# Routed attention in blocks of two rows of queries: 256 columns per instruction for values and sums

## The chip, the cores and the metric

One core of a Trainium2 chip runs the whole program. The metric is the time of one execution on the device in microseconds. Its engines are named as the profile names them: PE is TensorE (matmuls; PEld is its weight load), DVE is VectorE, ACT is ScalarE, POOL is GpSimd, SP is SyncE, which here only starts transfers.

## What is computed

The input x is 2 x 1024 tokens of 512 numbers. It is normalised, and two attentions are added to it: a local one with its own projections (16 query heads, 4 key heads, a window of 64 keys), and a routed one, which is what the change touches. In the routed attention each token has 16 query heads of 32 numbers but one key and one value only, those of the head that a gate picks:

```python
k_shared = einsum('bth,bthd->btd', indicator, k)
v_shared = einsum('bth,bthd->btd', gating_top1, v)
att = einsum('bhqd,bkd->bhqk', q, k_shared) * (1.0 / sqrt(32))
att = softmax(where(causal, att, -inf), axis=-1)
y = einsum('bhqk,bkd->bhqd', att, v_shared)
...
return x + local_attention(xn) + y
```

## The kernel before

The program has two stages. The first (0 to about 403 us) makes projections and the local attention of all tokens, 256 tokens a round. The second is the routed attention, from about 403 us to the end. It works through 8 units (`UNITS_ROUTED`), each a batch and a group of four heads (`HQ = 4`). A unit has 8 rows of queries, 128 queries each (`i`), against key blocks of 128 keys (`j`, up to `i`): 36 pairs, listed in `PRODUCTS` as (i, i), (i, 0), ..., (i, i-1).

For every unit PE does these kinds of work; the letters are used from here on.

- M, `row_scores` (L980): queries of one head by up to 512 keys into one of four PSUM banks (`s_ps`). DVE takes the causal maximum of each (L1250). There are 48 of them in a unit, written with 256, 384 or 512 columns. They are for the unit that comes next.
- ROW, `max_in_rows` (L994): once DVE has joined a unit's maxima (`row_maxima`, L1270 to L1275), PE turns them into a row, ACT copies it and sends it by DMA (L1452) into the rows of `q_op` under the queries. The key scores of that unit wait for it.
- S, `key_scores` (L1011): 128 keys by 4 heads x 128 queries, 512 columns, into one of three banks (`st_ps`). ACT takes the exponential (L1469) into one of 12 buffers (`p_t`, `RING`). On the diagonal POOL clears what is not causal (L1589); of two neighbouring pairs of a row POOL makes the sum (L1600, `PAIR_OF`), into one of 6 buffers (`p_sum`, `SUMS`).
- V, `key_values` (L1025): for one pair, four matmuls (one for each head, 32 output partitions each) of `v_all` with the weights, into the one bank `od_ps`, 128 columns.
- v, `key_sums` (L1039): the same with a block of ones in place of the values, for each sum of two pairs, at the end of a row. In this trace every matmul of V and v stands as two records, two passes for each operand of four bytes, and the four heads of a pass run side by side.
- F, `finish` (L1049): after ACT has copied `od_ps` (L1479), two transposes; DVE divides (L1287, L1289) and after rows 3 and 7 adds what the first stage left (L1296).

All engines run one list of steps in order. The class `Routed` writes that list by a model of its own: it keeps a time for each engine and always takes the step that could start first, in the order F, M or ROW, S, V where they tie. V goes in groups: `value_group` takes 4 pairs at once, or all that are left in the row if these are 5 or fewer, and the sums follow the row's last group. `TURN = 0.15` is what the model counts for entering and for leaving such a group. It counts 0.22 us for the four matmuls of one pair:

```python
        for g in range(k, k + value_group(k)):
            self.do("key_values", u, b, g)
            self.now += 0.22
```

No step waits out of order: what PE's list puts behind a ROW waits for that ROW. The functions that the diff touches:

## Time and profile before

| what | value |
|---|---|
| median of 3 runs | 728.02 us (725.67 to 728.77) |
| the profiled execution, its own time | 726.53 us |
| its span from first to last instruction | 725.1 us |
| mean granted clock of TensorE | 0.969 |
| first stage | to about 403 us |
| ROW of units 1 and 7 | 458.2 and 683.9 us |

The profile is one execution. A granted clock of 1.00 is 2.4 GHz, 0.50 is 1.2 GHz. In the timeline an entry may hold several instructions; the start of the next entry says when the engine went on, since busy times of pipelined matmuls overlap. In the order lists below one line is one run of like instructions.

### The profile page before, as it was taken

The numbers are of one execution on the slowest core, as the hardware profiler recorded it, in microseconds if no ns is written. First come the engines' busy times: TensorE is split into PE (matmuls) and PEld (weight loads), VectorE is DVE, ScalarE is ACT, GpSimd is POOL, SyncE is SP. The second block draws the span as 40 slices with busy tenths as digits, with TensorE's granted clock in tenths as the row PEclk, the third lists the DMA queues.
The fourth block names the chain that finished last, engine by engine and source line by source line (L and its number), as shares of the span: only waits on it lengthen the run. The fifth ranks groups of instructions, "written<-read, shape, count | busy, mean of one in ns | idle before, by whom it ended". The sixth has DMA issues, their size and how long they took to land. (4 is left out here: it accounts for less than half of the span.)

```text
span 725.1 us, 19425 instructions
## 1 busy us (share of the span) xinstructions
PE 660.7 (91%) x7433; PEld 522.8 (72%) x7433; DVE 528.7 (73%) x1376; ACT 365.0 (50%) x907; POOL 432.4 (60%) x352
## 2 busy tenths in 40 slices
PE   4796999899989999989988889899999999999997
PEld 3675887778877888778876567676767676667775
DVE  3975677577783777837865898898888888988621
ACT  4453454426545255443454235356556555656674
POOL 2963846285671856707752236466766666767696
PEclk9899999999999999989999789899999999999999
DMA  8412122232211322112116500311413130402011
GB/s 295 178 57 87 45 63 87 71 88 68 82 46 55 102 63 73 59 55 74 54 49 185 142 24 24 104 45 48 104 47 86 47 101 26 126 26 82 4 32 31
DMA packets 61451, 55.04 MB, mean 76 GB/s; under 512 B 5806, under 2 KB 52270, under 8 KB 61358
## 3 DMA queue, kind: packets, MB, share of 16 engines
q1 hardware_dynamic: 59096, 52.76, 24.4%
q8 instruction: 59, 0.97, 0.6%
q10 hardware_dynamic: 2262, 1.04, 0.5%
q14 instruction: 34, 0.28, 0.1%
HBM read 35.63 MB, written 17.89 MB: 74 GB/s over the span
## 5 line engine op out<-in xcount | busy, mean ns | idle before, releaser
L1250 DVE CUSTOM_DVE_ANT_0 s_ps<-s_ps,x_ln 128x512 f32<-128x512 f32 (+2 forms) x368 | 196.2, 589 | 34.0 <-PE s_ps L980 32.7
L862 PE MATMUL gemm<-w_tok,xt 128*128 128x512 f32 (+1 forms) x768 | 179.6, 382 | 4.7 <-DVE g_exp L1110 2.3
L862 PEld LDWEIGHTS gemm<-w_tok,xt 128*128 128x128 f32 x768 | 132.9, 194 | 29.8 <-DVE g_exp L1110 2.8
L980 PE MATMUL s_ps<-k_stack,w_tok 96*128 96x512 f32 (+2 forms) x368 | 117.9, 407 | 2.2 <-DVE picked_fk L1250 1.6
L1011 PE MATMUL st_ps<-w_tok,k_stack 98*128 98x512 f32 x288 | 105.1, 430 | 0.4 <-ACT qkv L1469 0.2
L1469 ACT ACTIVATE p_loc<-st_ps 128x512 f32<-128x512 f32 x144 | 77.8, 599 | 46.6 <-PE st_ps L1011 46.1
L980 PEld LDWEIGHTS s_ps<-k_stack,w_tok 96*128 96x128 f32 x368 | 65.4, 200 | 35.4 <-DVE picked_fk L1250 17.1
L1416 ACT ACTIVATE p_loc<-win,l_max 128x96 f32<-128x96 f32 x256 | 61.1, 391 | 12.4 <-DVE l_max L1195 12.4
L1547 POOL TENSOR_TENSOR rope_b<-qkv,sin_t 128x128 f32<-128x128 f32 (+1 forms) x32 | 27.4, 879 | 65.2 <-DVE qkv L1162 65.1
L1469 ACT ACTIVATE p_loc_t<-st_ps 128x512 f32<-128x512 f32 x96 | 52.2, 599 | 24.2 <-PE st_ps L1011 23.4
L1531 POOL TENSOR_TENSOR rms_y<-rms_v,minus_half 128x20 f32<-128x20 f32 x16 | 58.6, 3666 | 9.4 <-DVE rms_v L1172 9.4
L858 PE MATMUL gemm<-xt,w_qt 128*128 128x256 f32 x384 | 57.6, 296 | 5.4 <-DVE picked_fv L1141 3.4
L1011 PEld LDWEIGHTS st_ps<-w_tok,k_stack 98*128 98x128 f32 x288 | 52.4, 198 | 10.8 <-ACT p_loc L1469 2.3
L858 PEld LDWEIGHTS gemm<-xt,w_qt 128*128 128x128 f32 x384 | 51.0, 197 | 8.9 <-DVE picked_fv L1141 4.5
L1571 POOL TENSOR_TENSOR p_loc<-p_loc,l_rec 128x1536 f32<-128x1536 f32 x16 | 44.2, 2761 | 22.0 <-DVE l_rec L1207 22.0
L948 PE MATMUL gemm<-w_o,attn_t 128*128 128x512 f32 x192 | 50.5, 398 | 2.3 <-DVE x_res L1221 1.7
L1250 DVE DVE_READ_ACCUMULATOR2_ANT picked_fk<- 128x1 f32 x368 | 51.6, 140 | 0.0
L1589 POOL TENSOR_SCALAR_AFFINE_SELECT p_loc<-p_loc 128x512 f32<-128x512 f32 x40 | 25.3, 638 | 42.9 <-ACT p_loc L1469 42.8
L1425 ACT ACTIVATE p_loc_t<-win 96x512 f32<-96x512 f32 x64 | 37.5, 604 | 19.8 <-PE win L922 19.7
L922 PE MATMUL win<-idt,p_loc 128*96 128x128 f32 x256 | 40.9, 286 | 5.4 <-ACT p_loc L1416 4.9
L1025 PE MATMUL od_ps<-p_loc,v_all 128*32 128x128 f32 x1152 | 44.6, 278 | 0.0
L948 PEld LDWEIGHTS gemm<-w_o,attn_t 128*128 128x128 f32 x192 | 34.6, 188 | 9.2 <-DVE x_res L1221 2.0
(155 smaller groups left out, 1244.8 us busy)
## 6 DMA issues: line engine op xcount, KB each, us to landing
w_tok<-q_parts SPq DMA_DIRECT2D x96, 128.0 KB, 2.6
q_parts<-qt SPq DMA_DIRECT2D x64, 128.0 KB
x_ln<-x SPq DMA_DIRECT2D x8, 512.0 KB, 6.3
x_res<-x SPq DMA_DIRECT2D x16, 256.0 KB, 5.0
partial<-x_res SPq DMA_DIRECT2D x16, 256.0 KB, 2.1
k_t<-partial SPq DMA_DIRECT2D x8, 512.0 KB, 5.4
raw<-w_tok SPq DMA_DIRECT2D x3, 1024.0 KB, 13.0
v_win<-v_rows SPq DMA_DIRECT2D x64, 48.0 KB, 2.7
```

Source lines behind the costliest of these rows:

```text
L858: i = e.matmul(g[:, 0:PAIR], w_qt_p[r][:, k, a * P:(a + 1) * P], xs[l][:, k, :], start=first, stop=last)
L862: i = e.matmul(g[:, 0:cols], xs[l][:, k, a * P:(a + 1) * P], w_tok_p[r][:, k, c0:c0 + cols], start=first, stop=last)
L922: i = e.transpose(win[0:KEYS, quad, g * P:(g + 1) * P], p_loc[a][:, g, quad, :], idt[:, :])
L948: i = e.matmul(gemm[bank][:, :], attn_t[l][:, kc, :], w_o_p[r][:, kc, :], start=kc == 0 and q == 0, stop=kc == KC - 1 and q == 2)
L980: e.matmul(s_ps[bank][:, 0:cols], q_op[b][0:HALVES, h, i * P:(i + 1) * P], k_stack[0:HALVES, b * S + c0:b * S + c0 + cols], start=True, st ...
L1011: e.matmul(st_ps[k % ST_BANKS][:, :, :], k_stack[0:HALVES + 2, b * S + j * P:b * S + (j + 1) * P], q_op[b][0:HALVES + 2, :, i * P:(i + 1) ...
L1025: mm = e.matmul(od_ps[h * DK:(h + 1) * DK, 0, :], v_all[:, b * IT + j, 0:DK], p_t[k % RING][:, h, :], start=i == j, stop=ends_row(k))
L1250: e.tensor_tensor_reduce(out=s[:, 0:cols], in0=s[:, 0:cols], in1=causal[:, S - width + c0:S - width + c0 + cols], scale=1.0, scalar=NEG, o ...
L1416: i = e.activation(p_loc[a][:, g, quad, :], win[:, g, quad * KEYS:(quad + 1) * KEYS], ACT.Exp, bias=l_max[:, a, n:n + 1])
L1469: e.activation(p_t[k % RING][:, :, :], st_ps[k % ST_BANKS][:, :, :], ACT.Exp, scale=ROUTED_SCALE).then_inc(*M["rp_exp"].did((u, k)))
L1531: e.tensor_tensor(rms_y[:, :], rms_v[:, :], minus_half[:, :].to_broadcast([P, NH]), ALU.pow).then_inc(*M["rms_r"].did((n, a)))
L1571: e.tensor_tensor(p_l, p_l, l_rec[:, a, :].unsqueeze(2).to_broadcast([P, H, KEYS]), ALU.mult).then_inc(*M["p_r"].did((m, a)))
```

## The change

Two rows of queries (2c and 2c+1) are now one block row `c`, four in a unit. `BLOCKS` lists (c, j) with the two diagonal key blocks first: 2 + 4 + 6 + 8 = 20 blocks. Scores are still 36 instructions of 512 columns, but one instruction now holds 2 heads x 256 queries (`part` 0 and 1); for j = 2c+1, which only the second row sees, it holds 4 heads x 128 as before (`part` 2). Values take four matmuls of 256 columns for 16 blocks of a unit and four of 128 for the other 4. Sums are taken for the two diagonal blocks by themselves and for pairs of the others, 14 in a unit where there were 20; POOL makes 12 sums of pairs in a unit instead of 16, and clears 12 diagonal pieces (8 of 256 elements, 4 of 512) instead of 8 of 512. `od_ps` is copied 4 times instead of 8, at 512 columns; F is 4 transposes, 4 times in a unit. `RING` goes from 12 to 18 and `SUMS` from 6 to 9, in rooms of `v_win`, `k_t`, `x_res` and `picked_fv`; what the first stage left is read into the room of `w_qt`. `VALUES_AT_ONCE` stays 4, now counted in blocks, and the model still counts 0.22 us for a block.

```diff
-PRODUCTS = [(i, j) for i in range(IT) for j in (i, *range(i))]
-RING = 12
+CP = IT // 2
+BLOCKS = [(c, j) for c in range(CP) for j in (2 * c, 2 * c + 1, *range(2 * c))]
+
+SCORES = [(n, part) for n, (c, j) in enumerate(BLOCKS) for part in ((2,) if j > 2 * c else (0, 1))]
+PIECES_OF = [[k for k, (m, _) in enumerate(SCORES) if m == n] for n in range(len(BLOCKS))]
+RING = 18
...
+    if BLOCKS[_n][1] < 2 * BLOCKS[_n][0] and BLOCKS[_n][1] % 2:
...
+SUMS = 9
...
-def value_group(k):
+def value_group(n):
 
-    left = row_end(PRODUCTS[k][0]) - k + 1
+    left = block_end(BLOCKS[n][0]) - n + 1
     return left if left <= VALUES_AT_ONCE + 1 else VALUES_AT_ONCE
...
-        for g in range(k, k + value_group(k)):
-            self.do("key_values", u, b, g)
+        for m in range(n, n + value_group(n)):
+            self.do("key_values", u, b, m)
             self.now += 0.22
...
-            self.values_free = self.copied[u * IT + i] = self.busy(self.now + 0.1, ("A", 0.38)) + HOP
+            self.values_free = self.copied[u * CP + c] = self.busy(self.now + 0.1, ("A", 0.6)) + HOP
...
-        self.now += 0.25
-        self.s_free[bank] = self.busy(self.now + 0.1, ("V", 0.5)) + HOP
+        self.now += 0.45
+        self.s_free[bank] = self.busy(self.now + 0.1, ("V", 0.65)) + HOP
...
-                e.matmul(st_ps[k % ST_BANKS][:, :, :], k_stack[0:HALVES + 2, b * S + j * P:b * S + (j + 1) * P],
-                         q_op[b][0:HALVES + 2, :, i * P:(i + 1) * P], start=True, stop=True).then_inc(
-                             *M["rst_mm"].did((u, k)))
+                if part == 2:
+                    queries = q_op[b][0:HALVES + 2, :, (2 * c + 1) * P:(2 * c + 2) * P]
+                else:
+                    queries = q_op[b][0:HALVES + 2, 2 * part:2 * part + 2, 2 * c * P:(2 * c + 2) * P]
...
                 for h in range(HQ):
-                    mm = e.matmul(od_ps[h * DK:(h + 1) * DK, 0, :], v_all[:, b * IT + j, 0:DK],
-                                  p_t[k % RING][:, h, :], start=i == j, stop=ends_row(k))
-                mm.then_inc(*M["rpv"].did((u, k)))
+                    k = PIECES_OF[n][0 if j > 2 * c else h // 2]
+                    if j > 2 * c:
+                        to, weights = od_ps[h * DK:(h + 1) * DK, 0, P:2 * P], by_head(p_t[k % RING], 2)[:, h, :]
+                    else:
+                        to, weights = od_ps[h * DK:(h + 1) * DK, 0, :], by_head(p_t[k % RING], 0)[:, h % 2, :]
+                    mm = e.matmul(to, v_all[:, b * IT + j, 0:DK], weights, start=j == 2 * c, stop=ends_rows(n))
+                mm.then_inc(*M["rpv"].did((u, n)))
...
-                for h in range(2):
-                    mm = e.transpose(turned_back(u, i)[:, h, :], o_sb[i % 2][:, h, :], idt[:, :])
-                mm.then_inc(*M["ro_mm"].did((u, i)))
+                for n in range(4):
+                    mm = e.transpose(turned_back(u, c)[:, n, :], o_sb[c % 2][:, n, :], idt[:, :])
+                mm.then_inc(*M["ro_mm"].did((u, c)))
```

The first place in the order is the seam between two units on PE, around the ROW of unit 3 (`s_ps<-idt,picked_fk`). `st_ps` rows are S, `od_ps` rows are V and v, the other `s_ps` rows are M. Before:

```order
L1025 MATMUL od_ps<-p_loc,v_all 32x128 x4
L1011 MATMUL st_ps<-w_tok,k_stack 128x512 x2
L994 MATMUL s_ps<-idt,picked_fk 64x128
L980 MATMUL s_ps<-k_stack,w_tok 128x256 x2
L1011 MATMUL st_ps<-w_tok,k_stack 128x512
L980 MATMUL s_ps<-k_stack,w_tok 128x256
L1025 MATMUL od_ps<-p_loc,v_all 32x128 x12
L1039 MATMUL od_ps<-bias_o,v_all 32x128 x4
```

After:

```order
L993 MATMUL s_ps<-k_stack,w_tok 128x512
L1029 MATMUL st_ps<-w_tok,k_stack 128x512 x5
L1007 MATMUL s_ps<-idt,picked_fk 64x128
L993 MATMUL s_ps<-k_stack,w_tok 128x256 x8
L993 MATMUL s_ps<-k_stack,w_tok 128x384 x4
L1029 MATMUL st_ps<-w_tok,k_stack 128x512 x2
L993 MATMUL s_ps<-k_stack,w_tok 128x512
L1029 MATMUL st_ps<-w_tok,k_stack 128x512
L993 MATMUL s_ps<-k_stack,w_tok 128x512
L1048 MATMUL od_ps<-qkv,v_all 32x256 x4
```

Before, the ROW stands among the last S of the running unit, and V, v and S of that unit follow it. After, all S of the running unit stand ahead of the ROW, twelve small M follow it, and the next two S are the first of the unit whose row it brings; the V group of the running unit's end comes behind them. This stands so at the ROWs of units 3 to 6. At that of unit 2 the V group follows eleven small M, ahead of the S; at that of unit 7 it follows the ROW at once, since no M is left.

The second place is PE near the end, in unit 7, where no M is left. Before, rows 1 and 2 of the unit:

```order
L1011 MATMUL st_ps<-w_tok,k_stack 128x512 x3
L1049 MATMUL s_ps<-idt,rope_b 128x128 x2
L1025 MATMUL od_ps<-p_loc,v_all 32x128 x4
L1039 MATMUL od_ps<-p_loc,v_all 32x128 x4
L1011 MATMUL st_ps<-w_tok,k_stack 128x512 x3
L1049 MATMUL s_ps<-idt,rope_sq 128x128 x2
L1025 MATMUL od_ps<-p_loc,v_all 32x128 x8
L1039 MATMUL od_ps<-bias,v_all 32x128 x4
```

After, block rows 0 and 1:

```order
L1076 MATMUL s_ps<-idt,rope_b 128x128 x4
L1029 MATMUL st_ps<-w_tok,k_stack 128x512 x4
L1048 MATMUL od_ps<-p_loc,v_all 32x256 x4
L1048 MATMUL od_ps<-p_loc,v_all 32x128 x4
L1066 MATMUL od_ps<-p_loc,v_all 32x256 x4
L1066 MATMUL od_ps<-p_loc,v_all 32x128 x4
L1029 MATMUL st_ps<-w_tok,k_stack 128x512 x3
L1076 MATMUL s_ps<-idt,rope_sq 128x128 x4
L1029 MATMUL st_ps<-w_tok,k_stack 128x512 x7
L1048 MATMUL od_ps<-p_loc,v_all 32x256 x4
```

Before, never more than three S stand together there; after, runs of 4, 7, 7 and 5 do.

## Rows read from the trace of the kernel before

**Rows 1.** The page, part 1: busy time, share of the span, instructions.
```profile
PE 660.7 (91%) x7433; PEld 522.8 (72%) x7433; DVE 528.7 (73%) x1376; ACT 365.0 (50%) x907; POOL 432.4 (60%) x352
```

**Rows 2.** Stretches: us, busy PE, PEld, DVE, ACT, POOL (instructions), clock, DMA.
```profile
534.00:572.00 38.00, 36.64 (x567) 27.03 (x568) 32.86 (x123) 21.48 (x44) 25.10 (x24) 1.00 0.26 73
686.00:725.00 39.00, 33.63 (x661) 24.75 (x660) 7.68 (x23) 25.65 (x53) 30.86 (x28) 0.99 0.11 30
```

**Rows 3.** Line L994, the ROW: its records in the stage.
```profile
L994 PE MATMUL s_ps<-idt,picked_fk x8: 269/270/272, 425.3 to 683.9; 128*64 128x128 f32 x7, 128*32 128x128 f32 x1
```

**Rows 4.** Waits of PE, 475 to 675 us: total, times, longest.
```profile
PE s_ps L994 <- DVE picked_fk L1275: 6.2, 5, 1.4
PE s_ps L1049 <- DVE picked_fk L1250: 2.2, 4, 0.8
```

**Rows 5.** Timeline of PE, 560 to 572 us: start, us, engine, line, count.
```profile
560.81 0.40 PE L1011 MATMUL st_ps<-w_tok,k_stack 98*128 98x512 f32 x1
561.14 0.86 PE L1025 MATMUL od_ps<-p_loc,v_all 128*32 128x128 f32 x24
561.82 0.40 PE L1025 MATMUL od_ps<-p_loc_t,v_all 128*32 128x128 f32 x8
562.15 1.19 PE L980 MATMUL s_ps<-k_stack,w_tok 96*128 96x512 f32 x4
563.18 0.63 PE L1011 MATMUL st_ps<-w_tok,k_stack 98*128 98x512 f32 x2
563.65 0.45 PE L980 MATMUL s_ps<-k_stack,w_tok 96*128 96x512 f32 x1
...
564.73 0.40 PE L1039 MATMUL od_ps<-cos_t,v_all 128*32 128x128 f32 x8
564.95 0.40 PE L1039 MATMUL od_ps<-sin_t,v_all 128*32 128x128 f32 x8
```

**Rows 6.** Timeline of PE at the lower clock, 453 to 470 us.
```profile
467.11 0.65 PE L1025 MATMUL od_ps<-p_loc,v_all 128*32 128x128 f32 x8
467.53 0.65 PE L1039 MATMUL od_ps<-p_loc,v_all 128*32 128x128 f32 x8
```

**Rows 7.** Line L1025: idle of its engine ahead of it, us and times.
```profile
  issue: 22.6, 78
```

**Rows 8.** Timeline of PE, 453 to 470 us: the ROW of unit 1, the next S.
```profile
458.15 0.27 PE L994 MATMUL s_ps<-idt,picked_fk 128*64 128x128 f32 x1 [1.13 <-DVE picked_fk L1275]
...
461.69 0.80 PE L1011 MATMUL st_ps<-w_tok,k_stack 98*128 98x512 f32 x1 [0.22 <-DMA w_tok<-w_tok]
```

**Rows 9.** Timeline of DVE, 419 to 430 us: maxima of small M.
```profile
421.19 0.73 DVE L1250 CUSTOM_DVE_ANT_0 s_ps<-s_ps,x_ln 128x512 f32<-128x512 f32 x1
...
421.84 0.73 DVE L1250 CUSTOM_DVE_ANT_0 s_ps<-s_ps,x_ln 128x512 f32<-128x512 f32 x1
...
426.23 0.29 DVE L1250 CUSTOM_DVE_ANT_0 s_ps<-s_ps,x_ln 128x128 f32<-128x128 f32 x1
...
429.23 0.59 DVE L1250 CUSTOM_DVE_ANT_0 s_ps<-s_ps,x_ln 128x384 f32<-128x384 f32 x1
```

**Rows 10.** Stretches around ROWs, columns as in the stretches above.
```profile
427.30:434.10 6.80, 6.80 (x17) 5.30 (x18) 6.16 (x24) 2.96 (x6) 3.19 (x3) 0.50 0.02 4
...
458.00:461.40 3.40, 2.63 (x11) 1.65 (x11) 2.53 (x15) 0.27 (x1) 0.00 (x0) 1.00 0.03 10
461.40:468.30 6.90, 6.68 (x31) 4.90 (x31) 5.74 (x21) 3.63 (x7) 4.35 (x5) 0.51 0.79 209
...
529.70:533.10 3.40, 2.17 (x37) 1.17 (x35) 3.23 (x8) 2.66 (x5) 1.98 (x3) 1.00 0.00 0
```

**Rows 11.** Timeline, 683.5 to 725.2 us: a run of S, and the end.
```profile
691.02 1.97 PE L1011 MATMUL st_ps<-w_tok,k_stack 98*128 98x512 f32 x4 [0.23 <-ACT qkv L1469]
...
717.77 1.28 POOL L1600 TENSOR_TENSOR sin_t<-qkv 128x512 f32<-128x512 f32 x1
...
719.60 0.38 ACT L1479 ACTIVATE rope_b<-od_ps 128x256 f32<-128x256 f32 x1 [2.22 <-PE od_ps L1039]
```

More of the change, by code:

```diff
@@ L526, in next_scores @@
             if n >= 0:
-                whats.append(self.done.get(("pair used", n)))
+                w, was = divmod(n, len(PAIR_OF))
+                whats.append(self.done.get(("sum", w, SUMMED_IN[was])))
         return None if None in whats else max(whats)
     def take_scores(self):
-        u, k = divmod(self.scored, len(PRODUCTS))
+        u, k = divmod(self.scored, len(SCORES))
         _, hg, b = self.unit(u)
-        i, j = PRODUCTS[k]
+        n, part = SCORES[k]
+        c, j = BLOCKS[n]
         self.do("key_scores", u, b, k)
@@ L537, in take_scores @@
         self.st_free[k % ST_BANKS] = end + HOP
-        if i == j:
-            end = self.busy(end + HOP, ("G", 0.64))
+        if on_diagonal(n):
+            end = self.busy(end + HOP, ("G", 0.64 if part == 2 else 0.38))
         self.done["weights", self.scored] = end + HOP
@@ L542, in take_scores @@
             end = self.busy(end + HOP, ("G", 1.3)) + HOP
-            self.done["pair", self.scored] = self.done["pair", self.scored - 1] = end
-        if (i, j) in ((2 * c + 1, 2 * c) for c in range(IT // 2)) and u + B < UNITS_ROUTED:
-            self.do("q_load", *self.unit(u + B), i // 2)
-            self.q_ready[u + B, i // 2] = self.now + 3.0
+            self.done["pair", self.scored] = self.done["pair", self.scored - 2] = end
+        if k == last_scores(c) and u + B < UNITS_ROUTED:
+            self.do("q_load", *self.unit(u + B), c)
+            self.q_ready[u + B, c] = self.now + 3.0
@@ L560, in next_values @@
+        last = n + value_group(n) - 1
+        base = u * len(SCORES)
+        if base + PIECES_OF[last][-1] >= self.scored:
+            return None
+        whats = [self.done["weights", base + k] for m in range(n, last + 1) for k in PIECES_OF[m]]
+        if BLOCKS[n][1] == 2 * BLOCKS[n][0]:
             whats.append(self.values_free)
-        if ends_row(k + value_group(k) - 1):
-            whats += [self.done["pair", end - m] for m in (1, 2) if ("pair", end - m) in self.done]
+        if ends_rows(last):
+            whats += [self.done["pair", base + k] for k in PIECES_OF[last] if k in PAIR_OF]
@@ new lines, in tensor_program @@
+                if part == 2:
+                    queries = q_op[b][0:HALVES + 2, :, (2 * c + 1) * P:(2 * c + 2) * P]
+                else:
+                    queries = q_op[b][0:HALVES + 2, 2 * part:2 * part + 2, 2 * c * P:(2 * c + 2) * P]
+                e.matmul(by_head(st_ps[k % ST_BANKS][:, :], part),
+                         k_stack[0:HALVES + 2, b * S + j * P:b * S + (j + 1) * P], queries,
+                         start=True, stop=True).then_inc(*M["rst_mm"].did((u, k)))
+            elif step == "key_values":
+                u, b, n = key
+                c, j = BLOCKS[n]
+                if j == 2 * c and (c or u):
+                    lane.wait_ge(*M["ro_r"].of((u, c - 1) if c else (u - 1, CP - 1)))
+                if on_diagonal(n):
+                    lane.wait_ge(*M["rp_diag"].of((u, n)))
@@ L1278, in vector_program @@
             elif step == "finish":
-                u, hg, b, i = key
-                lane.wait_ge(*M["ro_mm"].of((u, i)))
-                values, sums = (turned_back(u, i)[:, n, :].rearrange("p (h d) -> p h d", h=HQ) for n in range(2))
-                rows = out_sb[b][:, i, :]
-                if i == 0 and hg:
-                    lane.wait_ge(*M[f"stored{b}"].of(hg - 1))
-                if i or u:
-                    lane.wait_ge(*M["ro_norm"].of((u, i - 1) if i else (u - 1, IT - 1)))
-                e.reciprocal(o_rec[:, :], sums[:, :, 0]).then_inc(*M["ro_rec"].did((u, i)))
@@ L1288, in vector_program @@
[L1288 to L1294 removed]
+                u, hg, b, c = key
+                lane.wait_ge(*M["ro_mm"].of((u, c)))
@@ new lines, in vector_program @@
+                values, sums = (turned_back(u, c)[:, 2 * n:2 * n + 2, :].rearrange("p r (h d) -> p (r h) d", h=HQ)
+                                for n in range(2))
+                if c == 0 and hg:
+                    lane.wait_ge(*M[f"stored{b}"].of(hg - 1))
+                if c or u:
+                    lane.wait_ge(*M["ro_norm"].of((u, c - 1) if c else (u - 1, CP - 1)))
+                e.reciprocal(o_rec[:, :], sums[:, :, 0]).then_inc(*M["ro_rec"].did((u, c)))
+                lane.wait_ge(*M["ro_rec"].of((u, c)))
```

241 lines of the change are left out of this document (118 added, 123 removed).

## The prediction

> **What bounds the kernel now.** I read the page's busy times first: PE is busy for 91% of the span, DVE for 73% [rows 1]. A share of the span mixes stages, so next the stretches of the routed stage, which alone is changed: in a stretch of 38 us in its middle PE is busy for 36.6 us, DVE for 32.9, POOL for 25.1 and ACT for 21.5 [rows 2]. The reader should see that PE is first and DVE a close second, with little room for either to wait for the other. From the ROW of unit 1, at 458.15 us [rows 8], to that of unit 7, at 683.9 us [rows 3], six units pass: (683.9 - 458.15) / 6 = 37.6 us for one. After the last M DVE is nearly idle (7.7 of 39 us) and PE is busy for 33.6 [rows 2]. So what lengthens or shortens PE's list, or makes PE wait, counts almost in full in all eight units. The waits of PE with a name are small: 6.2 us in five units at the ROW, 1.24 us each, and 2.2 us at F [rows 4].
>
> **What the timeline says of a V group.** Two passes of V or v (an entry of x8) take 564.95 - 564.73 = 0.22 us, so 0.109 us for a pass of 128 columns by four heads [rows 5]. At half the clock two passes take 467.53 - 467.11 = 0.42 us, 0.21 for one, twice as long [rows 6]. A cost of issuing instructions would not double with the array's clock, so the columns set this time, and a pass of 256 columns costs two of 128. I take 0.216 us; the bounds are 2 x 0.105 = 0.210, half of the row at the lower clock doubled, and 2 x 0.109 = 0.218. The Trainium skill ("TensorE: Matmul & The Clock Gate", section "Wait — 56ns, not 53.3ns?") gives a warm matmul a fixed cost of about 2.5 ns besides its columns. By that rule alone, 352 fewer passes would gain 352 x 2.5 ns = 0.9 us, far less than halving the passes suggests; the trace has no pass of 256 columns to check it on.
>
> Entering and leaving a group costs more. From the S at 560.81 to that at 563.18 us are 2.37 us [rows 5]. They hold eight passes (x24 and x8), 0.87 us, and five matmuls of 512 columns, 0.235 us each by the pair at 563.18 and 563.65: 1.18 us. The rest is 0.32 us. PE's weight loader shows it too: 22.6 us of "issue" idle before 78 groups, 0.29 us each [rows 7].
>
> **The change, part by part.** All of it is on the path, by the above, where nothing else is said.
>
> 1. Columns of V and v. Before: 8 x (36 + 20) = 448 sets of four matmuls, two passes each: 896 x 0.109 = 97.7 us. After: of 8 x (20 + 14) = 272 sets 208 have 256 columns and 64 have 128: 416 x 0.216 + 128 x 0.109 = 103.8 us. That is +6.1 us (+3.7 to +7.0): V has the same columns but for rounding, and v has more, since the diagonal blocks are no longer paired.
> 2. Groups. Before, rows of 1 to 8 pairs make 11 groups a unit, and one is merged: 87. After, block rows of 2, 4, 6 and 8 make 6: 48. 39 x 0.32 = -12.5 us (39 x 0.29 = -11.3, with 0.34 -13.3).
> 3. The seams at the ROWs of units 3 to 6. After, five S stand ahead of the ROW: three go at once, the last two wait for ACT, whose exponentials come every 0.49 us (x4 in 1.97 us [rows 11]): 0.5 us of waiting. The ROW then waits for DVE's last maxima, about 0.4 us by my count. Then comes the row itself: 461.69 - 458.15 = 3.54 us from ROW to the S that needs it [rows 8]. PE has twelve small M for this, eight at about 0.12 and four at 0.18 us: 1.6 us by their columns at 0.235 us for 512. DVE allows that: it starts nine such maxima in 429.23 - 426.23 = 3.0 us [rows 9], and four banks run ahead. The S waits 1.9 us. In sum 2.8 us, against 1.24 of before and some 0.3 beside it: +1.3 each, +5.2 us for four. Bounds: 0, if the row comes while PE still waits for DVE, and 4 x 2.0 = 8, if it shares its transfer with the loads of queries that SP starts at the same moment. Before, V, v and S of the running unit lay behind the ROW and hid all this.
> 4. The other ROWs. Longer V groups stand ahead of those of units 0, 1 and 2, and PE reaches them later or waits longer: +0.8, +0.5, +0.5 = +1.8 us (0 to 3), estimates from the order.
> 5. F. The transposes are as many. Half as many F waits for a bank: 2.2 us in five units [rows 4] is 3.5 in eight, so -1.5 us with some left (0 to -2).
> 6. The clock. After the ROW of unit 1, whose S has to wait for the row with eight M and an F in between, the granted clock is 0.51 for 6.9 us [rows 10]. After the change two more M stand there. At the full clock the work would take half, 3.4 us less. I take a gain of 1.4 us for it (0 to 3.4).
> 7. The tail. With no M left, S runs at ACT's pace as soon as more than three stand together: 0.49 instead of 0.235 us. Before, unit 7 has only runs of three. After, it has 3 and 4 around an F, then 3 and 7, a 7, and a 5: by the pace above about 1.0 + 1.6 + 1.0 + 0.5 + 0.3 = 4.4 us of waiting, against some 1.4 of before (the run of four at 691.02 [rows 11]): +3.0 us (0 to +5). At the very end POOL adds two parts instead of one, 1.28 us each [rows 11], mostly under V and v; the copy has twice the columns (0.38 before), F two transposes more, DVE twice the elements: +0.9 us (0 to 1.6).
>
> What costs nothing: ACT's exponentials are as many; POOL makes 32 sums of 1.28 us fewer and had 8 of 39 us free even in the last stretch; DVE has 32 divisions fewer. These engines had room in the stretches [rows 2], so I gain nothing from them either; if the cover went, it would be DVE's (rival 3). The 18 buffers hold more pieces than one block row has, 15.
>
> Sum: +6.1 - 12.5 + 5.2 + 1.8 - 1.5 - 1.4 + 3.9 = +1.6 us. The profiled execution took 726.53 us, so 728.1; it lies 1.5 us under the median of the runs, so **729.6 us** beside 728.02. All the low ends together make -15.0 us and all the high ones +13.3, that is 713 and 741; they won't all fall together.
>
> **Rivals.** Less than 0.5% (3.6 us) can't be told from no change here, so faster means under 724.4 and slower over 731.7.
>
> *1. The waits are absorbed.* What terms 3 and 4 charge was there before in other guise, since DVE is second in line: a PE that comes later finds banks free. Then +6.1 - 12.5 - 1.5 - 1.4 + 0.9 = -8.4 us: 719.6. For it speaks that all M and all waits for them are DVE's pace; against it that 3.54 us from ROW to S is a transfer and no engine's queue.
>
> *2. The clock falls at each new seam.* This is the rival on the slow side that I fear. In the trace PE drops to half the clock just after ROWs that are followed by small M alone: from 427.3 and from 461.4 us, 6.8 and 6.9 us long. Where S, V and v stand around the ROW, as at 529.7 to 533.1 us, with a wait as long, it stays at 1.00 [rows 10]. The new order has the first pattern at four more ROWs. If all four fall, 4 x 3.4 = +13.6 us: 743. Each fall takes 3.4 us; two of them already make the kernel slower. Against it: twelve M stand there, not eight, and five S just ahead, so PE does more in the stretch than it did at 458 us. The Trainium skill ("TensorE: Matmul & The Clock Gate", section "HAM oscillation — how this bites in real kernels") describes such a kernel, whose PE falls back at every wait between bursts of work; the trace agrees at two ROWs and not at the later ones.
>
> *3. DVE becomes the bound.* The last group of a unit is now 4 x 0.43 for V and 4 x 0.43 + 0.22 for v, about 3.7 us without an M, where the longest was 8 x 0.22 = 1.75. Four banks of maxima last 4 x 0.65 = 2.6 us (421.84 - 421.19 [rows 9]), so DVE runs dry for about 1.1 us a unit. It has 5 us of room in 38 [rows 2] and loses some 1.2 us of work in F, so I expect no loss; if the room is not there, 8 x 1.1 less what it saves is up to +6 on top: 730 to 737.
>
> *4. A pass costs the same whatever its columns.* Then 448 sets become 272, -38 us. The doubling at half the clock [rows 6] excludes it nearly.
>
> **How the numbers follow.** My forecast 0.45 (alone 723 to 736 us; of it 0.06 is faster, 0.28 same, 0.11 slower), absorbed waits 0.26, the clock 0.19, DVE 0.08 (half same, half slower), the fixed pass 0.02. Faster: 0.06 + 0.26 + 0.02 = 0.34. Same: 0.28 + 0.04 = 0.32. Slower: 0.11 + 0.19 + 0.04 = 0.34. Range 717 to 742: it leaves out the fixed pass, the lowest quarter of the absorbed waits and about half of the clock's case, some 0.18.
>
> **What would show it.** Passes of V with 256 columns 0.216 us apart; about 48 entries of PEld "issue" before L1048. At the ROWs of units 3 to 6 PE idle, released by the DMA of the row, for some 2 us; an interval of units near 37.6 us. Granted clock: falls near 427 us, none from 470 us on. S in unit 7 in runs released by ACT. I am wrong if the S after the ROW doesn't wait (faster by 5 us), or if the clock shows 0.50 after the middle ROWs.

## The result, and the profile after

The changed kernel takes **755.69 us** in the median of its runs, beside 727.83 us for the kernel before on the same chip: a ratio of 1.036 (95% interval 1.033 to 1.040). One of its four runs took 3042.57 us; without it the median is 754.08 us, and the ratios, here and below, leave such a run out, while the printed medians hold it. By the ratio the loss is 26 us (0.0362 x 728); between the two profiled executions it is 27.5 us. It is nearly twice the loss of the slow rival (743 us), and outside my range.

The profiled execution took 754.08 us. Parts 1 and 2 of its page (busy time by engine; then PE and the granted clock in 40 slices):

```profile
PE 683.5 (91%) x6025; PEld 506.7 (67%) x6025; DVE 521.4 (69%) x1312; ACT 356.8 (47%) x875; POOL 395.6 (53%) x352
...
PE   4797999899979999799887898989899998989896
...
PEclk9799999999999999899997998989889897989999
```

Against [rows 1] PE has 1,408 instructions fewer and yet 23 us more of busy time; DVE, ACT and POOL all have less. The clock row tells why one must look at the second half of the span, where 8 and 9 alternate (9 stands for 0.9 or more, 8 for less). Next the whole routed stage, of the kernel before and then of the one after (us, PE, PEld, DVE, ACT, POOL, clock, DMA):

```profile
403.00:725.00 322.00, 302.69 (x4376) 220.39 (x4376) 251.88 (x904) 178.33 (x361) 205.58 (x192) 0.96 0.21 58
```

```profile
403.00:752.00 349.00, 324.84 (x2969) 203.11 (x2969) 245.85 (x841) 170.75 (x329) 169.69 (x192) 0.91 0.19 54
```

All of the loss is here: 27 us. PE's busy time grew by 22.2 us and its idle time by 4.9. (A wait under 0.2 us between two matmuls counts as busy here, and so does work at the low clock.) The ROWs say where in the stage. Their line after, beside [rows 3]:

```profile
L1007 PE MATMUL s_ps<-idt,picked_fk x8: 270/272/395, 426.3 to 710.8; 128*64 128x128 f32 x7, 128*32 128x128 f32 x1
```

Seven units pass between first and last ROW: (710.8 - 426.3) / 7 = 40.6 us each, where it was (683.9 - 425.3) / 7 = 36.9. That is 25.9 of the 27.5 us by which the span grew. The first ROW came 1.0 us later, and what follows the last one takes 41.8 us instead of 41.2. So the loss lies in the units, and the single ROWs tell in which. They start at 426.3, 461.0, 498.5, 540.7, 583.8, 625.6, 668.8 and 710.8 us; up to the ROW of unit 2 the changed kernel has lost 2.5 us, and after that each unit costs it 3.5 to 5.8 us more than the same unit before. From the ROW of unit 3 on a unit takes (710.8 - 540.7) / 4 = 42.5 us, where it took (683.9 - 533.2) / 4 = 37.7.

The seam at the ROW of unit 3, PE's timeline (start, us, engine, line, operation, count; in brackets the idle time ahead and what ended it):

```profile
536.68 0.86 PE L1029 MATMUL st_ps<-w_tok,k_stack 98*128 98x512 f32 x3
537.76 0.99 PE L1029 MATMUL st_ps<-w_tok,k_stack 98*128 98x512 f32 x2 [0.22 <-ACT v_win L1499]
540.74 0.39 PE L1007 MATMUL s_ps<-idt,picked_fk 128*64 128x128 f32 x1 [1.99 <-DVE picked_fk L1302]
540.87 4.25 PE L993 MATMUL s_ps<-k_stack,w_tok 96*128 96x256 f32 x12
544.92 1.05 PE L1029 MATMUL st_ps<-w_tok,k_stack 98*128 98x512 f32 x2
...
547.18 1.08 PE L1048 MATMUL od_ps<-qkv,v_all 128*32 128x256 f32 x8
548.04 1.08 PE L1048 MATMUL od_ps<-v_win,v_all 128*32 128x256 f32 x8
...
551.39 0.38 PE L1066 MATMUL od_ps<-v_win,v_all 128*32 128x256 f32 x2
...
551.61 0.38 PE L1066 MATMUL od_ps<-bias_o,v_all 128*32 128x256 f32 x2
```

Three things stand in it. The ROW waits 1.99 us for DVE. The next S comes 544.92 - 540.74 = 4.18 us after the ROW, behind twelve M. And up to 550.4 us everything takes twice as long: two passes of V take 548.04 - 547.18 = 0.86 us, though one takes 551.61 - 551.39 = 0.22 us a little later. The stretches with the low clock (columns as above):

```profile
461.70:468.50 6.80, 6.49 (x17) 4.98 (x18) 6.20 (x28) 2.35 (x4) 1.45 (x3) 0.50 0.64 175
499.20:506.00 6.80, 6.76 (x44) 3.77 (x48) 4.22 (x22) 0.00 (x0) 0.33 (x1) 0.50 0.02 6
540.20:550.40 10.20, 9.62 (x50) 6.36 (x54) 6.72 (x29) 1.95 (x4) 3.03 (x5) 0.50 0.23 72
584.60:591.40 6.80, 6.75 (x30) 4.40 (x33) 6.13 (x28) 1.68 (x3) 1.63 (x4) 0.50 0.12 33
625.50:635.70 10.20, 10.06 (x54) 6.56 (x58) 6.32 (x28) 1.95 (x4) 2.58 (x4) 0.50 0.20 61
669.90:676.70 6.80, 6.76 (x29) 4.46 (x33) 5.89 (x26) 1.68 (x3) 1.45 (x3) 0.50 0.03 8
```

With 403.7 (10.2 us), 431.0 (3.4) and 710.9 (3.4) these are all in the stage while PE works: 65 us at 1.2 GHz. The kernel before has only those at 403.4 (10.2), 427.3 and 461.4 [rows 10], 24 us. Every ROW of units 2 to 7 now has a fall at it.

DVE at the same seam shows why the ROW waits:

```profile
536.99 0.70 DVE L1277 CUSTOM_DVE_ANT_0 s_ps<-s_ps,x_ln 128x512 f32<-128x512 f32 x1 [0.54 <-PE s_ps L993]
...
537.85 1.24 DVE L1297 TENSOR_TENSOR picked_fk<-picked_fk 128x16 f32<-128x16 f32 x1
539.12 0.18 DVE L1299 TENSOR_SCALAR picked_fk<-picked_fk 128x32 fp32r<-128x32 f32 x1
539.34 1.25 DVE L1302 SCALAR_TENSOR_TENSOR picked_fk<-picked_fk 128x32 fp32r<-128x32 f32 x1
```

The same of POOL:

```profile
537.78 1.27 POOL L1629 TENSOR_TENSOR picked_fv<-qkv,v_win 128x512 f32<-128x512 f32 x1 [0.61 <-ACT v_win L1499]
539.25 2.53 POOL L1629 TENSOR_TENSOR x_res<-k_t 128x512 f32<-128x512 f32 x2 [0.19 <-ACT k_t L1499]
```

Two DVE steps on 16 and 32 elements take 1.24 and 1.25 us, as long as POOL's sums, and end with them: 537.85 + 1.24 = 539.09 beside 537.78 + 1.27 = 539.05, and 539.34 + 1.25 = 540.59 beside 539.25 + 2.53 / 2 = 540.52. The step between them takes 0.18: it starts in the gap between two sums. It is so at nearly every ROW, and in the kernel before at some (least, median and longest time of the first of the two steps, after and then before):

```profile
L1297 DVE TENSOR_TENSOR picked_fk<-picked_fk x8: 174/1242/1247, 424.4 to 708.0; 128x16 f32<-128x16 f32 x8
```

```profile
L1270 DVE TENSOR_TENSOR picked_fk<-picked_fk x8: 175/528/1236, 424.6 to 682.8; 128x16 f32<-128x16 f32 x8
```

That the five S in a row ahead of the ROW put POOL's sums, which follow the exponentials, on DVE's joining steps is how I read the order; no run isolates it.

### The profile page after: what moved, and what is told of

The parts are those of the page before. It is cut to its first block, busy times and chain, and to the rows that moved or that the text cites. A ratio compares the mean times of both kernels' runs of the same rounds, so it can differ in the third digit from the quotient of the medians.

```text
span 752.6 us, 16284 instructions
## 1 busy us (share of the span) xinstructions
PE 683.5 (91%) x6025; PEld 506.7 (67%) x6025; DVE 521.4 (69%) x1312; ACT 356.8 (47%) x875; POOL 395.6 (53%) x352
## 3 DMA queue, kind: packets, MB, share of 16 engines
q10 hardware_dynamic: 2262, 1.04, 0.5%
## 4 chain that ended last, share of the span: by engine, by line
PE 45%; DVE 6%; issue 2%; ACT 1%; DMA 1%; POOL 0%; SPq 0%; DVEq 0%; ACTq 0%
PE s_ps L993 13%; PE od_ps L1048 10%; PE st_ps L1029 9%; PE od_ps L1066 6%; PE s_ps L1076 2%; PE gemm L875 2%; DVE picked_fk L1302 1%; PE gemm L961 1%; DVE s_ps L1277 1%; DVE picked_fk L1297 1%; DVE qkv L1207 1%; DMA q_parts<-qt 1%; PE win L935 0%; ACT p_loc L1443 0%; DVE l_sum L1231 0%
## 5 line engine op out<-in xcount | busy, mean ns | idle before, releaser
L1277 DVE CUSTOM_DVE_ANT_0 s_ps<-s_ps,x_ln 128x512 f32<-128x512 f32 (+2 forms) x368 | 194.7, 592 | 62.6 <-PE s_ps L993 61.1
L993 PE MATMUL s_ps<-k_stack,w_tok 96*128 96x512 f32 (+2 forms) x368 | 130.0, 434 | 3.2 <-DVE picked_fk L1277 1.2
L1029 PE MATMUL st_ps<-w_tok,k_stack 98*128 98x512 f32 x288 | 110.5, 437 | 1.8 <-ACT v_win L1499 1.5
L993 PEld LDWEIGHTS s_ps<-k_stack,w_tok 96*128 96x128 f32 x368 | 73.3, 215 | 44.2 <-issue 17.6
L1620 POOL TENSOR_SCALAR_AFFINE_SELECT p_loc<-p_loc 128x256 f32<-128x256 f32 (+1 forms) x72 | 35.1, 494 | 97.2 <-ACT p_loc L1499 94.7
L1499 ACT ACTIVATE p_loc<-st_ps 128x512 f32<-128x512 f32 x96 | 51.2, 603 | 48.2 <-PE st_ps L1029 47.8
L1029 PEld LDWEIGHTS st_ps<-w_tok,k_stack 98*128 98x128 f32 x288 | 56.0, 201 | 22.2 <-ACT v_win L1499 6.5
L1509 ACT ACTIVATE rope_b<-od_ps 128x512 f32<-128x512 f32 x16 | 9.6, 597 | 62.5 <-PE od_ps L1066 62.5
L935 PEld LDWEIGHTS win<-idt,p_loc 128*96 128x96 f32 x256 | 31.2, 132 | 10.9 <-issue 5.1
```

What stands on the lines that cost most here:

```text
L935: i = e.transpose(win[0:KEYS, quad, g * P:(g + 1) * P], p_loc[a][:, g, quad, :], idt[:, :])
L993: e.matmul(s_ps[bank][:, 0:cols], q_op[b][0:HALVES, h, i * P:(i + 1) * P], k_stack[0:HALVES, b * S + c0:b * S + c0 + cols], start=True, st ...
L1029: e.matmul(by_head(st_ps[k % ST_BANKS][:, :], part), k_stack[0:HALVES + 2, b * S + j * P:b * S + (j + 1) * P], queries, start=True, stop=T ...
L1277: e.tensor_tensor_reduce(out=s[:, 0:cols], in0=s[:, 0:cols], in1=causal[:, S - width + c0:S - width + c0 + cols], scale=1.0, scalar=NEG, o ...
L1499: e.activation(p_t[k % RING][:, :], st_ps[k % ST_BANKS][:, :], ACT.Exp, scale=ROUTED_SCALE).then_inc(*M["rp_exp"].did((u, k)))
```

## The experiments

The causes that stood against each other were the clock (falls at the seams), the hold-up of DVE's joining steps by POOL's sums, and the order alone (theory C): 256-column groups priced at 0.22 us in a model that decides who stands where. Medians are in us; ratios are to the kernel before, measured beside the version on the same chip, with 95% intervals. Since not all versions ran on one chip, differences between versions are taken between their ratios: 0.001 is 0.73 us, and an interval reaches up to 3.6 us to either side. The changed kernel is at 1.0362.

**e1 and e2: keep PE at work at the seam.** Six matmuls of 512 columns into the free bank ahead of the ROW, five ahead of the first S of a unit, nothing reads them; in the changed kernel (e1) and in the kernel before (e2).

```diff
-                lane.wait_ge(*M["r_lo"].of((u, part)))
...
+                    for _ in range(KEPT_ROW):
+                        e.matmul(s_ps[plan.turn["s", ("max_in_rows", u)]][:, :], k_stack[0:HALVES, 0:P],
+                                 k_stack[0:HALVES, 0:512], start=True, stop=True)
...
+                lane.wait_ge(*M["r_lo"].of((u, part)))
...
+                if k == 0 and u:
+                    lane.wait_ge(*M["rp_exp"].of((u - 1, len(SCORES) - ST_BANKS)))
+                    for _ in range(KEPT_SCORES):
+                        e.matmul(st_ps[0][:, :], k_stack[0:HALVES, 0:P],
+                                 k_stack[0:HALVES, 0:512], start=True, stop=True)
```

> The changed kernel with work added only: six matmuls of 512 columns into the bank that the ROW takes, ahead of the wait for DVE's maxima, and five into the first score bank, ahead of the wait for the row (their results are overwritten, so the output is the same). The waits stay, but PE is busy in them. If the fall of the clock at each seam is what costs (theory A), the granted clock stays at 1.00 from 470 us on and the time drops from 755.7 to 735-742 us. If the waits themselves cost and the clock is only a sign of them (theory B), the clock stays up and the time moves by under 4 us.

> The kernel before with the same added matmuls, as control. Its clock falls in the routed stage near 427 and 461 us only. Theory A: these go and some 3 to 6 us with them (722-725 us), less up to 1 us per ROW where the added matmuls (1.4 us each time) outlast the wait. Theory B: within 3 us of 727.8, or slower.

Measured: e1 747.3, 1.028 (1.024 to 1.032); e2 731.95, 1.007 (1.004 to 1.010). Stretches of e1, the stage, the place of the fall at the seam of unit 3, and a long one behind it:

```profile
403.00:745.00 342.00, 327.52 (x3049) 208.03 (x3047) 245.26 (x840) 170.24 (x328) 169.99 (x192) 0.97 0.20 54
540.20:550.40 10.20, 9.86 (x96) 6.35 (x97) 6.16 (x29) 1.87 (x5) 2.71 (x5) 1.00 0.21 64
504.00:680.00 176.00, 172.10 (x1663) 111.62 (x1655) 137.10 (x464) 91.43 (x177) 88.36 (x103) 1.00 0.24 64
```

From 504 us to PE's last matmul the clock is 1.00, and 5.9 of the 26 us come back (8.4 by the printed medians); the intervals of the two ratios just miss each other. That is more than theory B's 4 us, but 747.3 us is outside theory A's range too. The low clock shrank from 65 to 20 us. Work at half the clock takes twice its time, so this is worth up to half of the difference, 22 us. The added matmuls take part of it back: 83 of them, of 0.235 to 0.26 us, are 20 to 22 us of PE's time. The stage rows agree, roughly: PE's busy time without them is 306 to 308 us, 17 to 19 less than the 324.8 of the changed kernel, and its idle time fell from 24.2 to 14.5 us. In the kernel before, whose low clock shrank only from 24 to 10 us, they cost 4.9 us net, which is what theory B had said of e2. So the clock is a real part of the loss, and I estimate it at 6 us (the net gain of e1) to 20 (half of the 41 us of low clock that the changed kernel has beyond the kernel before). That it isn't all of it follows from this bound, not from e1's unit of 41.0 us, which holds 2.8 us of added matmuls.

**e3: short sums on POOL.** The sums of pairs in the last block row of a unit cover 8 of 512 columns, so part of the values' sums is left out.

```diff
+                w = slice(0, 8 if u and BLOCKS[n][0] == CP - 1 else HQ * P)
```

> The changed kernel with part of the computation left out: from unit 1 on POOL's sums of pairs in the last block row (6 of 12 in a unit) take 8 columns instead of 512. That frees POOL while DVE joins the maxima ahead of the ROW. Theory A2 (DVE's operations on two SBUF operands stand still while POOL adds): L1297 and L1302 take about 0.2 us each instead of 1.24, PE's wait at the ROW falls from 2.0 to about 0.3 us, the clock falls at fewer of the ROWs of units 3 to 6, and the time drops by 10 us or more. If DVE is merely late with the last maxima, both operations and the wait stay and the time moves by under 3 us.

Measured: 742.67, 1.020 (1.015 to 1.025). The joining steps of DVE and the ROW behind them:

```profile
533.27 0.18 DVE L1297 TENSOR_TENSOR picked_fk<-picked_fk 128x16 f32<-128x16 f32 x1
533.66 0.18 DVE L1299 TENSOR_SCALAR picked_fk<-picked_fk 128x32 fp32r<-128x32 f32 x1 [0.21 <-DVE picked_fk L1297]
533.88 0.19 DVE L1302 SCALAR_TENSOR_TENSOR picked_fk<-picked_fk 128x32 fp32r<-128x32 f32 x1
```

```profile
533.18 0.99 PE L1029 MATMUL st_ps<-w_tok,k_stack 98*128 98x512 f32 x2 [0.23 <-ACT v_win L1499]
534.21 0.27 PE L1007 MATMUL s_ps<-idt,picked_fk 128*64 128x128 f32 x1
534.48 0.59 PE L993 MATMUL s_ps<-k_stack,w_tok 96*128 96x256 f32 x3
535.27 2.92 PE L993 MATMUL s_ps<-k_stack,w_tok 96*128 96x256 f32 x9 [0.20 <-ACT w_tok L1470]
538.33 1.22 PE L1029 MATMUL st_ps<-w_tok,k_stack 98*128 98x512 f32 x2
```

With POOL out of the way the two steps take 0.17 to 0.19 us at all ROWs, and this ROW has no wait of 0.2 us or more: the hold-up is shown. Over the stage PE's waits at ROWs behind DVE's last step fell from 13.4 to 2.2 us. The whole gain is 12 us. It isn't all the waits' own: the low clock shrank too, from 65 to 44 us, and other waits grew (three of 0.5 to 0.6 us for the row's transfer at later seams, where the changed kernel has none). But a fall at this seam stays, at 538.4 us and for 3.4 us instead of 10.2, right behind the twelve M. So a wait at the ROW isn't needed for it: what stood ahead were M at DVE's pace, and no wait above 0.23 us. (The profile is that of e3's fastest run, 738.25 us, so its waits and its low clock are, if anything, below those of the median.)

**e4: honest prices.** The model counts 0.43 us for a block whose values or sums have 256 columns.

```diff
         for m in range(n, n + value_group(n)):
             self.do("key_values", u, b, m)
-            self.now += 0.22
+            self.now += 0.22 if BLOCKS[m][1] > 2 * c else 0.43
```

and the same for the sums.

> The changed kernel with two numbers of the planner's model: a block of 256 columns counts 0.43 us for its values and for its sums instead of 0.22 (0.22 where it has 128). The work is the same; only the list's order changes: from unit 3 on the ROW stands among the S of the running unit again and the V group behind it, as before the change. If the order at the seams causes the loss (theory C), there are no clock falls from 540 us on and the time is 725-735 us. If blocks of 256 columns cost by themselves (passes or longer groups), it stays above 745.

Measured: 741.1, 1.016 (1.011 to 1.021). Its stretch from 584 us, and its ROWs:

```profile
584.00:740.00 156.00, 146.84 (x1523) 89.30 (x1521) 94.95 (x334) 87.45 (x169) 88.86 (x99) 0.99 0.19 52
```

```profile
L1007 PE MATMUL s_ps<-idt,picked_fk x8: 269/270/272, 424.8 to 695.4; 128*64 128x128 f32 x7, 128*32 128x128 f32 x1
```

More than half of the loss goes with right prices: 14.6 us. The time lies between the two forecasts. Falls are left up to the seam of unit 4 (580.8 us), none behind 584.2; the low clock is 41 us in all. Units take (695.4 - 424.8) / 7 = 38.7 us, and 739.9 - 695.4 = 44.5 us follow the last ROW.

**e5: the wrong price alone.** The kernel before with 0.11 where it has 0.22, so that rows of one have the same error of two.

```diff
-            self.now += 0.22
+            self.now += 0.11
```

> The kernel before, rows of 128 queries and all, with the planner's model made wrong in the way it is wrong after the change: the values and the sums of a pair count 0.11 us instead of 0.22, half of what they take. Only the order changes: at some seams (ROWs of units 2, 3, 5 and 6) no S or V of the running unit is left behind the ROW, or only one group. Theory C (the order at the seams costs, and blocks don't matter): slower than 727.8 by 5 to 20 us, with clock falls in the middle of the stage. Theory D (it takes blocks of two rows to lose time): within 3 us of 727.8.

Measured: 729.57, 1.003 (1.001 to 1.006). An error of two in the price costs the old kernel some 2 us, not 15. So a wrong price alone (theory C) doesn't explain the loss. It costs more with blocks of twice the columns: 15 us in groups of four (e4), 11 in groups of two (e9 beside e8, below).

**e6 and e7: DVE joins nothing.** DVE's second maximum of a row starts from the first one's result, so that the joining step L1297 goes, and the rest (L1302) reads one operand from PSUM; in e4 (e6) and in the kernel before (e7).

```diff
-                dst = r_max_far[:, h, i - PART:i - PART + 1] if c0 else r_max[:, h, i:i + 1]
+                dst = r_max[:, h, i:i + 1]
+                if c0:
+                    lane.wait_ge(*M["rs_max"].of((u, t - 1)))
...
-                    scale=1.0, scalar=NEG, op0=ALU.add, op1=ALU.max, accum_out=dst)
+                    scale=1.0, scalar=dst if c0 else NEG, op0=ALU.add, op1=ALU.max, accum_out=dst)
```

> The changed kernel with the planner's true prices and, besides, DVE's steps ahead of the ROW without an operation on two SBUF operands: the maximum of the second 512 keys starts from that of the first (the join L1297 goes), and the rest of the rounding (L1302) takes its first operand from the PSUM bank that the ROW will use. Theory A2 (POOL's sums hold up DVE's operations on two SBUF operands): each step takes 0.2 us at every ROW, the ROWs of units 3 and 4, which waited 2.7 and 1.5 us after e4's change, come without such a wait, and the time falls from 741.1 to 730-736 us. If the steps only waited for something else, within 2 us of 741.

> The same change of DVE's steps made to the kernel before, as control and as a candidate. Its ROWs waited 1.3 to 1.7 us each, with one or two of the steps at 0.5 to 1.2 us. Theory A2: waits at the ROW fall below 1 us, and 4 to 8 us are gained (720-724). If ROWs wait for something else, within 2 us of 727.8.

Measured: e6 758.35, 1.042 (1.040 to 1.045), 19 us worse than e4; e7 737.95, 1.014 (1.011 to 1.017). Both lose, against both forecasts. The chain of maxima, each second one waiting for the first, is the likely price: over the stage DVE idles 63 us ahead of its maxima, where e4 has 59, and they take 215 us instead of 194. The other half of the edit is cleared by e11, which keeps it and doesn't lose. In e6:

```profile
L1282 DVE CUSTOM_DVE_ANT_0 s_ps<-s_ps,x_ln 128x512 f32<-128x512 f32 (+3 forms) x240 | 143.7, 628 | 39.2 <-PE s_ps L993 38.1
L1282 DVE CUSTOM_DVE_ANT_0 s_ps<-s_ps,x_ln,picked_fk 128x128 f32<-128x128 f32 (+3 forms) x128 | 71.5, 558 | 23.6 <-PE s_ps L993 7.8 <-issue 1.0
```

As a test of the hold-up these two runs say nothing; e11 does it without the chain.

**e8 and e9: groups of two.** `VALUES_AT_ONCE` 2 instead of 4, as many columns in a group as before the change: e8 with the prices of e4, e9 alone.

```diff
-VALUES_AT_ONCE = 4
+VALUES_AT_ONCE = 2
```

> The changed kernel with true prices (as e4) and groups of two blocks of values instead of four (VALUES_AT_ONCE 2), so that the columns of a group are those of a group before the change. It pays for some five more groups a unit, 0.32 us each, 1.6 us a unit. If the length of the groups (DVE and ACT running dry in them) costs, it gains more than that: 725-738 us. If not, it is slower than e4's 741.1 by up to 12 us.

> The changed kernel with VALUES_AT_ONCE 2 alone; the planner still counts 0.22 us for a block of 256 columns. At the ROWs of units 4 to 7 the list then still has all S of the running unit ahead of the ROW and nine small M behind it. If the order at the seams (theory C) is the main part of the loss and the groups' length a small one, it stays near e4 or above, 740-756 us. If the length of the groups is the main part, it comes near e8: under 735 us.

Measured: e8 727.18, 0.998 (0.995 to 1.001); e9 737.96, 1.013 (1.009 to 1.017), between its two forecasts. Shorter groups alone give back 17 us, right prices alone 14.6, both all of it. (e9 moves the ROW too: a V group stands right ahead of it, not five S.) ROWs of e8, and its whole stage:

```profile
L1007 PE MATMUL s_ps<-idt,picked_fk x8: 269/284/300, 426.6 to 681.4; 128*64 128x128 f32 x7, 128*32 128x128 f32 x1
```

```profile
403.00:726.00 323.00, 308.93 (x2969) 190.20 (x2969) 237.59 (x841) 172.68 (x329) 167.89 (x192) 0.95 0.21 58
```

A unit takes (681.4 - 426.6) / 7 = 36.4 us, and PE idles for 14.1 us in the stage, where the kernel before had 19.3 and the changed one 24.2. While PE works no fall of the clock comes after 503 us. These are the instructions of the changed kernel, 28 us faster: the order of the lists is all that differs. What the group length does shows on DVE, by its idle time ahead of its maxima (`CUSTOM_DVE_ANT_0`, part 5 of the pages): 34.0 us in the kernel before; 62.6, 62.5 and 58.9 with groups of four (changed kernel, e3, e4); 47.2 and 41.9 with groups of two (e9, e8). Right prices alone hardly move it.

**e10: the clock kept on e4.** The added matmuls of e1 in the order of e4.

> e4 (true prices, groups of four) with e1's added matmuls at every ROW and first S. e4's profile has falls of the clock in units 1 to 5 that cost some 14 us of half speed in matmuls. Theory A (the clock costs by itself): 728-736 us, since the added matmuls outlast the wait in the later units by about 1 us each. If the falls only mark waits that stay: 740 us or more.

Measured: 742.25, 1.018 (1.014 to 1.022), the same as e4. The expectation has this outcome for falls that only mark waits that stay. The traces don't bear that out. The low clock shrank from 41 to 17 us, and the clock is 1.00 from 475 to 680 us. PE's busy time in the stage went from 318.1 to 323.6 us with 20 to 22 us of added matmuls in it, so the rest of its work took at least 14 us less; its idle time fell from 18.8 to 13.0. PE's added work eats what the clock gives: an account from the traces, not a test.

**e11: the rest from PSUM, on e8.** The negated maxima go to a PSUM bank first, and L1302 becomes a step that reads one operand there and one in SBUF; the maxima are not chained, and the join L1297 stays.

```diff
-                e.scalar_tensor_tensor(maxima[:, 1, :, :].bitcast(F32R), src, -1.0, maxima[:, 0, :, :], ALU.mult,
-                                       ALU.subtract)
+                    e.tensor_scalar(turned, src, -1.0, None, ALU.mult).then_inc(*M["r_neg"].did(u))
...
+                    e.tensor_tensor(maxima[:, 1, :, :].bitcast(F32R), turned, maxima[:, 0, :, :],
+                                    ALU.subtract)
```

> e8 with one step of DVE changed: the rest of the rounded maxima (L1302, 1.17 us at the ROW of unit 2 in e8) takes the negated maxima from the ROW's PSUM bank, written there by one more step of 0.2 us, so that it has one SBUF operand. The join L1297 stays as it was, without e6's chaining of maxima. Theory A2: 0.2 us more at most ROWs, 1.0 us less at that of unit 2: 725-729 us, not to be told from e8, and the step at 0.2 us at every ROW. If e6's and e7's loss came from this step and not from the chaining: 732 us or more.

Measured: 725.66, 0.995 (0.992 to 0.997). The step's line in e8, with the least, median and longest time, and then its new form in e11:

```profile
L1302 DVE SCALAR_TENSOR_TENSOR picked_fk<-picked_fk x9: 175/193/1168, 402.9 to 680.2; 128x32 fp32r<-128x32 f32 x7, 128x16 fp32r<-128x16 f32 x2
```

```profile
L1309 DVE TENSOR_TENSOR picked_fk<-s_ps,picked_fk x7: 191/191/192, 458.4 to 678.1; 128x32 fp32r<-128x32 f32 x7
```

With one operand in PSUM the step takes 0.19 us at all seven ROWs, though it meets a sum at one only, that of unit 2, where e8's step takes 1.17 us. In this piece of e11 at that ROW (POOL, then DVE) POOL's sum runs from 496.21 to 497.50 us, and neither of the steps inside it is longer than usual, while the join, with both operands in SBUF, ends with the sums ahead of it (495.06 + 1.04 = 496.10 beside 493.54 + 2.52 = 496.06):

```profile
493.54 2.52 POOL L1640 TENSOR_TENSOR v_win<-qkv,v_win 128x512 f32<-128x512 f32 x2 [2.58 <-ACT v_win L1510]
496.21 1.29 POOL L1640 TENSOR_TENSOR bias<-k_t 128x512 f32<-128x512 f32 x1
```

```profile
493.86 0.42 DVE L1327 TENSOR_TENSOR x_res<-s_ps,picked_fk 128x256 f32<-128x256 f32 x1
495.06 1.04 DVE L1297 TENSOR_TENSOR picked_fk<-picked_fk 128x16 f32<-128x16 f32 x1
...
496.22 0.19 DVE L1306 TENSOR_SCALAR s_ps<-picked_fk 128x32 f32<-128x32 f32 x1
496.44 0.19 DVE L1309 TENSOR_TENSOR picked_fk<-s_ps,picked_fk 128x32 fp32r<-128x32 f32 x1
```

The ratio is 0.003 under e8's (2 us), with intervals that overlap: as forecast it can't be told from e8. In this order few steps meet a sum, so little was to be had.

**e12: e8 with matmuls added at the first seams only**, up to that of unit 2, where e8's clock still falls.

```diff
+KEPT_ROW, KEPT_SCORES, KEPT_UNITS = 6, 5, 2
```

> e8 with the added matmuls at the ROWs of units 0 to 2 and the first S of units 1 and 2 only, where e8's clock still falls (13.7, 3.4, 10.2 and 3.4 us at half speed, the first not to be reached by them). Theory A: 720-725 us, faster than both kernels. If the clock is only a sign of waiting: 727 us or more.

Measured: 724.09, 0.992 (0.989 to 0.995): the lowest of all, 0.8% under the kernel before, though e11's interval overlaps it. It is 4 us under e8, and the two intervals just miss each other. This is what theory A had forecast: the falls left while PE works, at 404.7 (10.2 us) and 432.0 (3.4), lie in the first 33 us of the stage, 14 us at 1.2 GHz against 31 in e8, with 28 added matmuls. Behind them:

```profile
475.00:504.00 29.00, 28.43 (x295) 17.51 (x283) 22.09 (x76) 13.67 (x27) 16.07 (x16) 1.00 0.14 43
504.00:680.00 176.00, 174.33 (x1756) 108.96 (x1755) 147.65 (x521) 101.06 (x193) 95.38 (x111) 1.00 0.24 66
```

## Why the prediction was wrong

Two steps failed. Term 6 and the choice against rival 2 took the clock for a gain of 1.4 us, where the low clock grew by 41 us, worth up to 20 us of loss. Term 3 put the ROW's wait behind DVE at 0.4 us, where it is 2.0. Besides, term 2's gain of 12.5 us, which the forecast needed to stay near zero, was not seen.

**What bounds the kernel** was right: PE's list and PE's waits. The whole loss came between ROWs.

**Term 1, the columns** (+6.1): right. A pass of 256 columns takes 0.22 us (v, 551.39 to 551.61 us), and 0.43 at half the clock.

**Term 2, the groups** (-12.5): not seen. Fewer groups should have made a unit shorter by 1.6 us less 0.8 for the columns. No version with groups of four shows it: even e4, at full clock behind 584.2 us, takes 38.05 us for each of its last two units, where the kernel before takes (683.9 - 458.2) / 6 = 37.6 in the mean and e8, with 10 groups a unit instead of 6, takes (681.4 - 608.1) / 2 = 36.65. A span of PE between other work, 0.32 us for each group, was taken out of one place of the trace and multiplied by the count. What took its place was measured, not explained: PE's weight loader still sits idle 67 times ahead of L1048, 18.8 us in all, against 78 times and 22.6 us [rows 7]. e9 even gains 17 us by adding groups.

**Term 3, the seams** (+1.3 each): mis-sized. I took "about 0.4 us by my count" for the ROW's wait behind DVE's last maxima. That count gave the two joining steps their usual 0.18 us. They took 1.24 and 1.25, since POOL's sums ran at that moment, and the wait became 2.0 us at each ROW (PE's waits, 475 to 675 us, beside [rows 4]):

```profile
PE s_ps L1007 <- DVE picked_fk L1302: 9.9, 5, 2.0
```

The kernel before has the same hold-up at some ROWs: its joining step takes 0.18 us at the least and 1.24 at the most, and I never asked for that line. So only part of the wait is new: over the stage PE waits 13.4 us at ROWs behind DVE's last step, beside 9.4 before. And the S came 4.18 us after the ROW (4.12 in e3, at full clock), not 3.54, and not as a wait for the row's transfer: the twelve M ahead of it, which I counted at 1.6 us by their columns, came at DVE's pace and filled all of it. I had DVE's pace in hand, nine such maxima in 3.0 us [rows 9], or 4.0 us for twelve, and didn't use it. In sum the seam of unit 3 holds 0.22 + 1.99 + 4.18 = 6.4 us, where I had 0.5 + 0.4 + 3.54 = 4.4: 2.0 us more.

**Term 6, the clock** (a gain of 1.4): wrong in sign, and by size the main failure. The fall at the ROW of unit 1 didn't shrink (6.8 us at 461.7). I gave rival 2, a fall at each new seam, a chance of 0.19 with four falls of 3.4 us lost each. It is what happened, and more: six new falls, at units 2 to 7 and not at four of them, of 3.4 to 10.2 us, 41 us more at 1.2 GHz in the stage. I had written against it that twelve M and five S keep PE at work; e3 shows a fall without a wait of 0.2 us at the ROW, so M at DVE's pace did not hold the clock. The Trainium skill ("TensorE: Matmul & The Clock Gate", section "HAM oscillation — how this bites in real kernels") tells of a kernel that waits 3 to 5 us between bursts and falls back each time. The trace has the same fall at a shorter wait, 2.0 us at the ROW, and e3 adds the case without such a wait.

**Terms 4, 5 and 7.** Up to the ROW of unit 2 the changed kernel lost 2.5 us, where term 4 had 1.8. F waits 1.5 us in the stage, beside 2.8 before: term 5 was near. The time behind the last ROW grew by 0.6 us instead of 3.9, but that is no test of term 7, since the order moved this ROW: 36 S stand behind it, and 43 before. In e4, where 43 do, it grew by 44.5 - 41.2 = 3.3 us, near the term. Its ground was weaker than its size: the text ahead of the prediction says that never more than three S stand together in unit 7 before, but the trace has seven in a row, three at 689.83 us and the four at 691.02 [rows 11].

**The rivals.** The first (waits absorbed, 719.6) and the fourth (fixed cost of a pass) are out. The third, DVE as the bound, isn't met as it was put: DVE is busy for 246 of 349 us. Its mechanism, DVE running dry in long groups, is there (62.6 us of idle time ahead of the maxima, 34.0 before). The second has the mechanism of the clock, and with 743 us against 755.7 too small a price; it lacked the falls at units 2 and 7, the length of the others (up to 10.2 us) and the hold-up.

**What is left open.** That the order of the lists makes the whole loss is shown, by e8. How it does so is shown in parts: the hold-up by e3, the clock's part by e1, and by e12 on another order. The shares can't be added up: the clock 6 to 20 us (e1), the hold-up with the falls that went with it 12 (e3), prices 14.6 (e4), group length 17 (e9), and the sum is 26. I read them as one chain, which no run tests as a whole: long groups with half their price let DVE run dry and bunch five S ahead of the ROW, POOL's sums then meet DVE's joins, PE waits, and the clock falls. Which of them matters most can't be told from these runs. Why a unit of e4 at full clock isn't shorter than before isn't settled either.

## What to carry to other kernels

A change that doubles the length of an instruction must double its price in whatever orders the work, and keep the time of a group, not its count of blocks; here mending these two numbers took away all of the loss (e8). When PE is first and the list has a seam where small matmuls are fed at another engine's pace, look for the clock there before counting microseconds of waits. And before pricing a tiny step by its usual duration, look at its longest one in the trace.
